# The expert tile stage of a one-core kernel, written out for its 71 tiles in place of loops with registers and jumps

## The reference: what is computed

```python
x = x + _layernorm(_L0_attn_ref(_layernorm(x), ...))   # a long convolution by FFT, skip term, layer norm
x = x + _layernorm(_L0_ffn_ref(_layernorm(x), ...))    # a mixture of 8 experts, 2 for each token
```

```python
z = _layernorm(x, ln_g, ln_b)
probs = softmax(z @ rW + rb)                # 8 experts
w = weights of the two best, normalised
hid = gelu(z @ W1[e] + b1[e])               # 256 -> 512
outs = hid @ W2[e] + b2[e]                  # 512 -> 256
out = x + sum over e of outs * w
```

## Time and profile before

| what | value |
|---|---|
| median of 3 runs | 596.23 us (595.38 to 596.32) |
| profiled execution | 598.88 us |
| its span, from the first to the last instruction | 597.0 us |
| instructions recorded | 13147 |
| PE busy, PEld busy | 477.8 us, 395.3 us |
| DVE, ACT, POOL busy | 443.5 us, 350.3 us, 338.7 us |
| mean granted clock of TensorE | 0.937 |

### The profile page before, as it was taken

One profiled execution on the slowest core, in us unless ns is written; L12 is line 12 of the kernel. 1 busy time (PEld: TensorE's weight loads), 2 busy tenths in 40 slices (PEclk: granted clock), 3 DMA queues, 4 the chain that ended last, 5 costly groups with the idle time before them and its releaser, 6 DMA issues.

```text
span 597.0 us, 13147 instructions
## 1 busy us (share of the span) xinstructions
PE 477.8 (80%) x2775; PEld 395.3 (66%) x2776; DVE 443.5 (74%) x1469; ACT 350.3 (59%) x788; POOL 338.7 (57%) x266
## 2 busy tenths in 40 slices
PE   0388899889999885795999999999999999999300
PEld 0138888777888773542797788798887888887200
DVE  6999786999889848347677777777767777777283
ACT  6992845475676567613465565565655565565365
POOL 0000567643778874660367667767666676666547
PEclk9998999989999986988999999999999999999855
DMA  6205700131335669724435444444444443443497
GB/s 183 101 1 205 289 1 1 59 137 47 131 126 168 199 199 326 238 100 126 152 66 79 67 67 72 71 70 71 64 68 71 71 68 65 70 64 51 61 402 284
DMA packets 50125, 69.95 MB, mean 117 GB/s; under 512 B 10160, under 2 KB 39728, under 8 KB 49584
## 3 DMA queue, kind: packets, MB, share of 16 engines
q1 hardware_dynamic: 34528, 51.81, 26.2%
q0 software_dynamic: 15568, 17.81, 17.9%
HBM read 37.90 MB, written 31.69 MB: 117 GB/s over the span
## 4 chain that ended last, share of the span: by engine, by line
PE 45%; DVE 21%; issue 11%; ACT 10%; POOL 5%; DMA 3%; SPq 3%; another core or an unknown queue 1%; POOLq 0%; DVEq 0%; ACTq 0%
PE psum L1436 14%; PE psum L1455 13%; PE psum L1445 5%; PE psum L1330 3%; PE psum L1423 3%; POOL acc L1254 3%; DVE st L702 2%; PE psum L1301 2%; DVE ws L896 2%; SPq L394 1%; PE psum L1288 1%; DMA y_rows<-yw,dst 1%; POOL y_rows L1231 1%; ACT dump L593 1%; PE psum L1350 1%
## 5 line engine op out<-in xcount | busy, mean ns | idle before, releaser
L1231 POOL DMA_INDIRECT y_rows<-yw,dst x71 | 115.7, 1630 | 66.1 <-issue 22.8
L1436 PE MATMUL psum<-ws,z_hl 128*128 x426 | 119.0, 415 | 3.4 <-DVE z_hl L1094 2.5
L1455 PE MATMUL psum<-ws,h_hl 128*128 x852 | 115.9, 285 | 0.1
L1455 PEld LDWEIGHTS psum<-ws,h_hl 128*128 128x128 f32 x852 | 103.5, 189 | 0.3 <-issue 0.3
L1218 POOL DMA_INDIRECT wt<-w_rows,widx x71 | 70.1, 987 | 44.1 <-issue 18.0
L652 ACT ACTIVATE hg<-hb 128x512 f32<-128x512 f32 x71 | 44.9, 632 | 85.1 <-DVE hb L1102 74.6
L1436 PEld LDWEIGHTS psum<-ws,z_hl 128*128 128x128 f32 x426 | 76.3, 190 | 20.3 <-issue 5.2
L1176 POOL DMA_INDIRECT z_rows<-zn,pos x64 | 68.9, 1076 | 27.2 <-issue 17.1
L1102 DVE TENSOR_TENSOR hb<-psum,b1r 128x512 f32<-128x512 f32 x71 | 49.1, 692 | 36.8 <-issue 34.5
L1330 PE MATMUL psum<-yf,it 128*128 128x256 f32 x256 | 60.9, 395 | 2.6 <-DVE r L945 2.6
L638 ACT ACTIVATE z_f<-psum,gb 128x128 f32<-128x128 f32 x142 | 56.0, 443 | 11.1 <-PE psum L1423 8.9
(11 more groups left out here) (206 smaller groups left out, 854.7 us busy)
## 6 DMA issues: line engine op xcount, KB each, us to landing
z_in<-z_rows SPq DMA_DIRECT2D x71, 129.0 KB
w_raw<-in_dram SPq DMA_DIRECT2D x16, 512.0 KB, 5.9
xs<-in_dram SPq DMA_DIRECT2D x8, 512.0 KB, 5.8
x_dram<-xs SPq DMA_DIRECT2D x8, 512.0 KB
y_rows<-zn SPq DMA_DIRECT2D x8, 512.0 KB, 3.3
yr<-y_rows SPq DMA_DIRECT2D x8, 512.0 KB, 6.7
out_dram<-acc SPq DMA_DIRECT2D x7, 512.0 KB, 4.5
b1r<-in_dram SPq DMA_DIRECT2D x8, 256.0 KB
```

Source lines behind the costliest of these rows:

```text
L1231: pool.indirect_dma_start(y_rows, bass.IndirectOffsetOnAxis(ap=dst[m][:, 0:1], axis=0), yw[m % 3][:, :], None, compute_op=ALU.add).then_in ...
L1436: last = TE.matmul(ps_h[q], z_hl[q][:, a, k], w_at(e1, c, k * F, F), start=n == 0, stop=n == 5)
L1455: last = TE.matmul(ps_y[q], h_hl[q][:, a, k], w_at(e2, c, 1024 + k * H, H), start=n == 0, stop=n == 11)
```

## The change

`tiles` becomes one Python loop over i from -2 to 71, so every part is written out with constants, on PE, DVE and ACT. SP's and POOL's loops are written out in the same way, and keep their order. The steps of a tile, the buffers, the semaphores and the order on each engine stay as they are. `expert` still reads the number from the table for each tile once, into a register, but keeps what it read, and nothing is read a second time.

```diff
-UNROLL = 6
...
-    def tiles(eng, part, peel=0):
+    def tiles(eng, part):
 
         loaded[eng.engine.name] = {}
-        for i in range(-2, 3 + UNROLL * peel):
-            part(i, i % 2, i)
-        with eng.Fori(peel, (TILES - 5) // UNROLL) as j:
-            loaded[eng.engine.name] = {}
-            for u in range(UNROLL):
-                part(j * UNROLL + (3 + u), (1 + u) % 2, u)
-        loaded[eng.engine.name] = {}
-        for i in range(TILES - 2, TILES + 1):
+        for i in range(-2, TILES + 1):
             part(i, i % 2, i)
...
     def live(t):
-        return not isinstance(t, int) or 0 <= t < TILES
+        return 0 <= t < TILES
...
     def slot(t, u, ahead):
 
-        return (t if isinstance(t, int) else u + 3 + ahead) % UNROLL
+        return t % 6
 
     def early(t, n=1):
 
-        return isinstance(t, int) and t < n
+        return t < n
...
-                if not (isinstance(t, int) and t < 2):
+                if t >= 2:
...
             sp.wait_ge(sem("order_ready"), 1)
-            load_z(6, 0)
-            load_z(7, 1)
-            release(1, 1)
-            with sp.Fori(3, (TILES - 3) // 2) as j:
-                load_z(j * 2 + 2, 0)
-                release(j * 2 - 4, 0)
-                load_z(j * 2 + 3, 1)
-                release(j * 2 - 3, 1)
-            load_z(TILES - 1, 0)
-            for t in range(TILES - 7, TILES):
+            for t in range(6, TILES):
+                load_z(t, t % 2)
+                if t > 6:
+                    release(t - 6, t % 2)
+            for t in range(TILES - 6, TILES):
                 release(t, t % 2)
...
-            tiles(act, part, 1)
+            tiles(act, part)
...
-            for t in range(7):
-                gather_w(t + 4, t % 2, (t + 4) % 6)
-                scatter_y(t, t % 2, t % 6)
-            with pool.Fori(1, (TILES - 5) // UNROLL) as j:
-                for u in range(UNROLL):
-                    gather_w(j * UNROLL + (5 + u), (1 + u) % 2, (5 + u) % 6)
-                    scatter_y(j * UNROLL + (1 + u), (1 + u) % 2, (1 + u) % 6)
-            for t in range(TILES - 4, TILES):
+            for t in range(TILES):
+                if t + 4 < TILES:
+                    gather_w(t + 4, t % 2, (t + 4) % 6)
                 scatter_y(t, t % 2, t % 6)
```

## The result

The changed kernel takes 590.38 us (median of 4 runs, 585.55 to 592.15), the one before, timed beside it, 596.28 us (4 runs, 595.38 to 597.95). The ratio is 0.9883 with a 95% interval of 0.9837 to 0.993: 5.9 us faster, where 7.9 us was forecast (588.3 us, range 581.5 to 594.5). The profiled execution took 590.15 us, its span is 588.3 us.

What follows compares the result with a forecast made beforehand. The prediction took the ring of ACT and DVE, not PE, as the bound. It summed 6.9 + 0.7 + 0.3 = 7.9 us saved from the 596.23 us median to 588.3 us, range 581.5 to 594.5 us.

Steps and rivals of the forecast that it cites:

- The ring of ACT and DVE: Expert tiles: z_f, z_hl, hb, hg, yw, next z_f close a lap of 3.73 us in which nobody waits for PE.
- The ring's issue: DVE's idle gap before hb: constant table address cuts 0.505 to 0.400 us a tile, 66 looped tiles, 6.9 us saved.
- ACT's jumps: z_f behind ACT's loop jump comes 0.08 us late; nine back edges removed, 0.7 us saved.
- PE's jumps and reads at nothing: PE's 1.2 us idle at ten places and its repeated expert reads: covered by the ring, so nothing saved.
- the bound reading: PE's timeline read alone: ten back edges cost 1.49 us each, 14.9 us; the prediction disbelieved it.
- rival 1: PE is the bound after all: back edges and the end give 15.6 us, 580.6 us; chance 5%.
- the end: Behind the loops, DVE's last hb waits 0.67 us for PE; 0.3 us saved, as scatters cover part.
- Code at nothing: Fetching written-out code throughout costs nothing, as PE kept 3.44 us a tile on new code in the first stretch.
- Rival 4: Fetches stall the ring: 15 blocks at 0.9 us lose 13.5 us, giving 601.8 us; chance 10%.
- The irregular stalls: Five places in the stage, like DVE's 0.95 us idle before L1116: kept unchanged, with ends of -6.7 and +3 us.
- rival 2: Another wait, PE or a load at 3.70 us a tile, replaces the ring: 3.3 us saved, 592.9 us; chance 10%.
- Rivals 2 and 5: Another wait sets the pace, 592.9 us, 10%; or nothing is saved, within 0.2%, 6%.

Runs made afterwards that it cites:

- DVE alone: Against the kernel before, only DVE's program written out, all other engines keeping their loops: 578.10 us, ratio 0.9896.
- the other four loops together: Against the kernel before, PE, ACT, SP and POOL written out, DVE keeping its loop: 584.09 us, ratio 0.9992.
- the early read: Against the changed kernel, DVE reads the next tile's expert number right behind the issue of hb: 563.44 us, ratio 0.9648 to the kernel before.
- the two kernels with the early read and a loop on PE: DVE's read moved behind hb: in the kernel before with all loops, 566.37 us; in the changed kernel with PE alone in its loop, 564.43 us.
- the padding of 12: Against the changed kernel, twelve semaphore increments added to DVE's program ahead of the expert tiles: 577.30 us (1 run).
- the second profiles: The kernel before and the changed kernel, each unaltered and profiled again on another chip: stages of 248.41 and 243.32 us.

## Why the prediction was right, and where it was not

**The bound: right.** The ring of ACT and DVE sets the pace, not PE. Shown four ways: the lap follows DVE's gap up (+0.63 us) and down (-0.10 us), with PE's loop undone and DVE's kept it doesn't move, and with the gap gone the lap stops at PE's 3.44 us.

**The ring's issue, 6.9 us: right.** The gap was to become 0.40 us and the z_f 3.63 us apart; they are 0.40 and 3.64 us. 66 x 0.100 = 6.6 us, and DVE alone gave 6.6 us. The cause given, the operation that works out the address, is what the rows of L307 and L299 show gone.

**ACT's jumps, 0.7 us: right in size on the lap.** z_f is 0.08 to 0.09 us late at ACT's back edges and no longer so with ACT written out; nine of them are 0.7 to 0.8 us. On the total it can't be told from nothing: the other four loops together gave 0.6 us.

**PE's jumps and reads at nothing: right, but the price behind them was not.** The ring was the cover, and with the early read, where it is gone, PE does set the pace, at 3.44 us a tile. What was wrong is the 1.49 us a back edge of the bound reading, which rival 1 took as a fixed price (15.6 us with the end). With PE as the bound and its loop kept, a back edge costs 0.1 to 0.3 us; the 1.2 us shrink and go as the ring's signals come earlier. The same error stands behind three of my expectations: DVE alone (1 to 3 us expected, 6.6 us measured) and the two kernels with the early read and a loop on PE.

**Code at nothing: this is the term that failed.** The step took the first 58 us, where PE kept its pace while it ran new code, as the case for all engines. But PE wasn't the bound; DVE was. On DVE an entry into a new block costs 0.35 to 0.37 us where it falls ahead of hb (0.46 us once with DVE alone, 0.71 us once with the padding of 12). Above the usual 0.403 us the raised gaps hold 1.6 us in the first profile of the change and 2.0 us in the second; 1.1 us (three places) and 1.4 us (four) of that stand at such entries, the rest in the gaps whose cause is open. Rival 4 had the mechanism, with 0.9 us a block at 15 places; it came to about 40% of its price a block, in three and four places, and didn't decide, since the gain was larger. The 0.53 us that it named as the point of decision was for 15 blocks, all on the ring. The Trainium skill (Runtime: NRT & Kernel Launch, Instruction fetch mechanics) says of such a crossing that it is "mostly hidden", and names the fetch that a jump out of the blocks held would cost as a reason to unroll. The first agrees with the trace, where most entries don't show. The case of the second doesn't arise here: with all loops kept, the instruction queues list nothing from 340 to 520 us, and the four programs other than DVE's lost their loops for 0.6 us.

**The end, 0.3 us: nothing.** The 0.67 us ahead of the last hb are gone:

```profile
540.79 0.69 DVE L1089 TENSOR_TENSOR hb<-psum,b1r 128x512 f32<-128x512 f32 x1 [0.40 <-issue]
542.38 0.68 DVE L1089 TENSOR_TENSOR hb<-psum,b1r 128x512 f32<-128x512 f32 x1
```

But from hb of tile 69 to the last scatter it is 11.75 us, after 11.73 us before (11.85 and 11.65 us in the second profiles). POOL's scatters, each 1.6 us and spaced by their own transfers, covered all of it. The scatter at the end of the queue:

```profile
552.54 1.55 POOL L1218 DMA_INDIRECT y_rows<-yw,dst  x1 [1.00 <-DMA y_rows<-yw,dst]
```

**The sum.** 7.9 us were forecast. The lap gave 6.6, the jumps 0.7, the end 0, and the raised gaps took 1.6 to 2.0 back: 5.3 to 5.7 us, against 5.9 and 6.0 us measured on the two chips. The stages of the second profiles, 5.1 us apart, fall short of that by up to 0.9 us, which stays open. The irregular stalls, kept in the sum at nothing, were right to keep: the 4.9 us that the first pair of profiles shows in the excess isn't in the medians. The upper end of the range, 594.5 us, follows from no term named: 588.3 + 3 is 591.3 us, and rival 2 with the same 3 us is 595.9 us.

**Rivals 2 and 5.** No other wait took the ring's place, and rival 2's lap of 3.70 us is the median of neither profile of the change. The signs that I had named came: PE waits for hg at 50 of 66 tiles, the first instruction queue has 16 packets more (17 forecast), and no hole of 1.2 us stands before L1405.

## What to carry to other kernels

Where several engines run in a ring, find the lap in which nobody waits for anybody, and look at the idle time for "issue" in it: a register read that a sequencer does right before the instruction that needs it costs its time at every lap, and moved behind the issue of a long instruction it costs nothing (15.3 us here, against 6.0 us for writing out every loop; 18.4 us with all loops kept). Idle time for "issue" at another engine's back edge says nothing of what the loop costs the kernel as long as that engine isn't the bound. And a single profiled execution can carry stalls that no other one has: profile the kernel before twice before giving them a cause.

## What was not expected of the hardware

- A read of a number from SBUF into a register costs DVE's sequencer 0.63 us in all: a load of 305 ns, a register operation of 190 ns, an assertion of 23 ns, and some 0.1 us between them.
- Ten jumps of a PE loop whose body holds six tiles, with their repeated reads, cost 1 to 3 us in all when PE is the bound, and stood beside 1.2 us of idle time each when it was not.
- In DVE's straight program a place about every 126 recorded instructions (seven tiles of 18, or six of 21) delays hb by 0.35 us where it falls into the gap ahead of it; it moves with instructions put ahead of it. On PE no such place was seen: in the kernel with the early read, where PE is the bound and its program straight, every lap of its first transposes from tile 5 on is 3.44 or 3.46 us.
